# Sixteen ranks through four overlapped stages: VectorE's dependent steps in pieces of one link, attention scores over 32 rows, and a new order of the steps

## The reference

```python
x = x + jnp.tanh(g_xattn[0]) * _L0_xattn_ref(_layernorm(x, axis=-1), ctx_1024, mask_BxS2_bk0, ...)
x = x + jnp.tanh(g_ffn[0]) * _L0_ffn_ref(_layernorm(x, axis=-1), L0_ffn_w_gate, L0_ffn_w_up, L0_ffn_w_down)
x = x + jnp.tanh(g_xattn[1]) * _L1_xattn_ref(_layernorm(x, axis=-1), ctx_1024, ctx_1024, L1_xattn_Wq, ...)
x = x + jnp.tanh(g_ffn[1]) * _L1_ffn_ref(_layernorm(x, axis=-1), L1_ffn_Wr, L1_ffn_br, L1_ffn_W1, ...)
```

## Time and profile before

| | |
|---|---|
| median of 3 runs | 1644.17 us (1643.66 to 1647.43) |
| the profiled execution's own time | 1642.42 us |
| its span | 1640.8 us |
| TensorE, VectorE, ScalarE busy | 85%, 68%, 61% of the span |

### The profile page before, as it was taken

One profiled execution on the slowest core, in us unless ns is written; L12 is line 12 of the kernel. 1 busy time (PEld: TensorE's weight loads), 2 busy tenths in 40 slices (PEclk: granted clock), 3 DMA queues, 4 the chain that ended last, 5 costly groups with the idle time before them and its releaser, 6 DMA issues.

```text
span 1640.8 us, 35711 instructions
## 1 busy us (share of the span) xinstructions
PE 1400.4 (85%) x11645; PEld 1072.6 (65%) x11646; DVE 1117.3 (68%) x2887; ACT 993.4 (61%) x2861; POOL 413.3 (25%) x560
## 2 busy tenths in 40 slices
PE   2567789989999889989998671999999999999994
PEld 1445556665666566656664430888888888888883
DVE  7977779899988999899986534344444454444452
ACT  1244778888888888888876760444445444455542
POOL 0101011211122211212111112334433444344442
PEclk9587999999999999999999975999999999999997
DMA  6020132112320223203220005551231412322214
GB/s 192 13 87 30 62 103 103 45 61 104 103 92 21 95 104 103 72 33 104 94 94 8 8 14 179 177 162 32 33 112 30 114 32 35 108 35 32 35 31 123
DMA packets 63158, 123.58 MB, mean 75 GB/s; under 512 B 13955, under 2 KB 51967, under 8 KB 58879
## 3 DMA queue, kind: packets, MB, share of 16 engines
q1 hardware_dynamic: 45743, 102.75, 18.0%
q0 software_dynamic: 17312, 19.56, 7.2%
HBM read 78.64 MB, written 48.04 MB: 77 GB/s over the span
## 4 chain that ended last, share of the span: by engine, by line
PE 52%; DVE 32%; ACT 8%; issue 5%; DMA 2%; POOL 1%; SPq 0%; DVEq 0%; ACTq 0%; POOLq 0%
PE bank L1401 15%; PE bank L1403 14%; PE bank L1402 14%; DVE b_mn L1121 4%; ACT b_ex L746 3%; PE bank L1483 2%; PE bank L1495 2%; DVE wm L1238 1%; DVE f_hs L1182 1%; DVE split_room L1265 1%; DVE wm L1190 1%; PE bank L1719 1%; DVE x L1176 1%; DVE wm L1196 1%; DVE wm L1201 1%
## 5 line engine op out<-in xcount | busy, mean ns | idle before, releaser
L1401 PE MATMUL bank<-split_room,wm 128*128 128x256 f16 x1152 | 314.9, 273 | 8.2 <-issue 6.8
L1378 DVE SCALAR_TENSOR_TENSOR split_room<-bank,b12e,split_room 128x256 f32<-128x256 f32 x288 | 138.2, 484 | 265.6 <-ACT split_room L900 260.8
L1402 PE MATMUL bank<-split_room,wm 128*128 128x256 f16 x1152 | 314.8, 273 | 0.0
L1403 PE MATMUL bank<-split_room,wm 128*128 128x256 f16 x1152 | 314.7, 273 | 0.0
L900 ACT ACTIVATE split_room<-bank,b12e 128x256 f32<-128x256 f32 x288 | 134.2, 470 | 196.0 <-PE bank L1403 194.2
L746 ACT ACTIVATE b_ex<-bank,b_mn 128x120 f32<-128x120 f32 x512 | 177.0, 361 | 36.9 <-DVE b_mn L1121 28.0
L1403 PE MATMUL bank<-wm,split_room 128*128 128x256 f16 x576 | 157.0, 273 | 0.0
L1401 PE MATMUL bank<-wm,split_room 128*128 128x256 f16 x576 | 157.0, 273 | 0.0
L1402 PE MATMUL bank<-wm,split_room 128*128 128x256 f16 x576 | 157.0, 273 | 0.0
L692 POOL DMA_INDIRECT acc<-split_room,m_cur x72 | 116.1, 1612 | 133.0 <-ACT split_room L914 106.1
L1483 PE MATMUL bank<-b_k,b_q 128*128 128x480 f32 x256 | 131.8, 597 | 14.6 <-ACT b_q L834 14.6
(11 more groups left out here) (356 smaller groups left out, 3616.3 us busy)
## 6 DMA issues: line engine op xcount, KB each, us to landing
split_room<-in_L_ffn_W SPq DMA_DIRECT2D x48, 512.0 KB, 8.0
wsplit<-split_room SPq DMA_DIRECT2D x16, 1536.0 KB, 6.6
wm<-wsplit SPq DMA_DIRECT2D x16, 1536.0 KB, 8.5
acc<-x SPq DMA_DIRECT2D x17, 256.0 KB, 2.2
xin<-in_x SPq DMA_DIRECT2D x16, 256.0 KB
rows<-r_row SPq DMA_DIRECT2D x16, 256.0 KB, 3.7
ct<-in_ctx SPq DMA_DIRECT2D x16, 120.0 KB
cb<-in_ctx SPq DMA_DIRECT2D x16, 120.0 KB, 2.6
```

The source lines that it names most:

```text
L1378: dve.scalar_tensor_tensor(m_h[:, c % 3], bank[c % 4][:, TILE:2 * TILE], b12e[:, p, 1, c:c + 1], m_s[:, c % 2], ALU.add, ALU.mult).then_in ...
L1401: pe.matmul(o, lh, rh, start=start, stop=False)
L1402: pe.matmul(o, ll, rh, start=False, stop=False)
L1403: return pe.matmul(o, lh, rl, start=False, stop=stop)
```

## The change

**One link per step.** Chained steps are cut at each wait, and every piece is a step of its own that the tables can place: `variances` becomes `stats`, `moments` and `guard` (`B.ln`, `B.ln_1`, `B.ln_2`), the quantisation becomes `F.qa`, `F.qa_1`, `F.qa_2`, `F.qb`, `F.qc`, `F.qc_1`, `F.p`, `F.p_1`, the routing `R.logit` to `R.logit_5` and `R.rank_0` to `R.rank_5` (with `R.rank`, which only waits). The instructions and their waits stay as they are.

**Scores over 32 rows.** In B two rounds (of four heads each, in neighbouring groups of 32 rows of the array) are issued together, as four products of 32 rows and 240 columns that go to the two banks in turn. The channels of the heads are laid out in another order for this: `b_k` holds two copies of the keys in place of eight, `b_k_` writes it with two ScalarE instructions over 128 partitions instead of eight over 32, and the queries' and keys' weights and biases are permuted when they are split in the ramp (`prep_b`, `head_order`: 16 pieces of 64 elements per weight half and matrix in place of two of 512). The bias `bqk` comes with eight small transfers instead of one. Both banks must be free before a pair starts, and both minima wait for the pair's end.

**New tables.** All three tables are written anew for every engine.

```diff
-        b_k = sb("b_k", [P, NK, 2, QUAD, S])
+        b_k = sb("b_k", [P, NK, 2, S])
...
             "DVE": ...
-                "F.p/1 F.d1/2 A.p0/0 A.p1/0 B.rx1/3 F.t/1 W2/1 B.p7/3 B.ln/2 B.o1/3 A.ot/0 B.out/3 R.ln/3 F.gu0/1 A.out/0 "
+                "B.s4/2 F.ht1/1 B.s5/2 F.ln/0 A.s0/-1 F.ln_1/0 R.rank_2/3 F.ln_2/0 W0/0 B.s6/2 F.qa/0 B.rx0/2 F.qa_1/0 "
...
             def b_k_(b, p):
                 held(act, B.k_mm, b + 1)
-                for j in range(QUAD):
-                    h = slice(PITCH * j, PITCH * (j + 1))
-                    for a in range(2):
-                        last = act.activation(b_k[h, :, a, j], bank[2][h, 0:NK * S].rearrange("p (c s) -> p c s", c=NK), ACT.Copy, scale=C[h, C_M + a:C_M + a + 1])
+                for f in range(2):
+                    last = act.activation(b_k[:, :, f], bank[2][:, 0:NK * S].rearrange("p (c s) -> p c s", c=NK), ACT.Copy, scale=C[:, C_M + f:C_M + f + 1])
                 last.then_inc(B.k, 1)
...
                         w = (wq1, wk1, wv1, wo1)[n_ - 1]
-                        split(st1[:, n_ - 1], w[:, 0], w[:, 1])
+                        if n_ > 2:
+                            split(st1[:, n_ - 1], w[:, 0], w[:, 1])
+                            return
+                        for c in range(2):
+                            for a in range(2):
+                                for k in range(NK):
+                                    k_ = slice(k, k + 1)
+                                    split(head_order(st1[:, n_ - 1, k_], c, a, True)[:, 0],
+                                          head_order(w[:, 0, k_], c, a, False)[:, 0], head_order(w[:, 1, k_], c, a, False)[:, 0])
...
             def variances(G, ch, source):
-                def stage(b, p):
+                def stats(b, p):
                     ch.start(b)
                     dve.wait_ge(source.done, b + 1)
...
+                def moments(b, p):
+                    ch.go_on(b)
                     ch.hold()
...
+                def guard(b, p):
+                    ch.go_on(b)
                     ch.wait()
...
                 def minima(k):
                     def stage(b, p):
-                        dve.wait_ge(G.s_mm, b * n + k + 1)
+                        dve.wait_ge(G.s_mm, b * n + (k + 1 if G is A else k // 2 * 2 + 2))
...
+                def pair(b, k0):
+                    if k0 == 0:
+                        pe.wait_ge(B.q, b + 1)
+                        pe.wait_ge(B.k, b + 1)
+                    else:
+                        pe.wait_ge(B.exp, b * n + k0)
+                    for e in range(NK):
+                        for k in (k0, k0 + 1):
+                            t, r = k // per, k % per
+                            h = slice(PITCH * r, PITCH * (r + 1))
+                            last = pe.matmul(sbks[k % 2][:, e * 2 * S:(e + 1) * 2 * S], q[h, e, t * P:(t + 1) * P], kk[h, e], start=True, stop=True)
+                            if e == NK - 1:
+                                last.then_inc(B.s_mm, 1)
```

More of the change, by code:

```diff
@@ L369, in gated_stack @@
         FIRST = {
-            "SP": ("B.load@0 W@0 A.load@2 B.load@1 A.load@3 W@1 A.load@4 W@2 B.load@2 B.out@0 W@3 R.rank@0").split(),
-            "POOL": ("A.ln@0 A.ln@1 F.ln@0 A.ln@2 F.ln@1 B.ln@0 A.ln@3 F.ln@2 B.ln@1 R.ln@0 A.ln@4 R.scatter@0").split(),
[7 rows of a table removed]
-                "R.logit@0 A.t@4 B.s0@1 B.s1@1 F.a0@2 B.t0@1 B.s2@1 B.t1@1").split(),
[11 rows of a table removed]
-                "R.rank@0 A.rk@4 B.s3@1 F.q1c@2 F.p1@2 F.ht0@2 B.s4@1").split(),
[8 rows of a table removed]
-                "B.t0@1 B.s2@1 B.p0@1 R.rank@0 A.kv@4 B.t1@1 F.ht0@2 B.t2@1 B.s3@1 A.q0@4 A.q1@4 B.p1@1").split(),
+            "SP": ("W@0 A.load@2 B.load@0 B.load@1 A.load@3 W@1 W@2 A.load@4 W@3 B.load@2 B.out@0 B.load@3 R.rank@0").split(),
@@ L444, in gated_stack @@
+            "POOL": ("R.ln@13 R.scatter@13 B.ln@15 R.ln@14 R.scatter@14 R.ln@15 R.scatter@15").split(),
[6 rows of a table added]
+                "B.t6@15 B.t7@15 B.rx1@15 B.r7@15 B.o1@15 R.z@15 R.t@15 R.logit@15").split(),
[11 rows of a table added]
+                "R.rank_4@15 R.rank_5@15 R.rank@15").split(),
[6 rows of a table added]
+                "B.p4@15 B.t5@15 B.t6@15 B.p5@15 B.t7@15 B.p6@15 B.p7@15 B.out@15 R.t@15 R.logit@15 R.rank@15").split(),
         }
@@ L1122, in minima, with shares @@
                     return stage
-                def values(k):
+                def shares(k):
                     def stage(b, p):
@@ L1137, in rounds @@
                 if G is A:
-                    made.update({f"{G.name}.p{k}": values(k) for k in range(per - 1, n, per)})
+                    made.update({f"{G.name}.p{k}": shares(k) for k in range(per - 1, n, per)})
+                    made.update({f"{G.name}.p{k}_1": values(k) for k in range(per - 1, n, per)})
                 return made
@@ new lines, in f_scale, with stage, f_inverse @@
+            def f_scale(n):
+                v, m, sc = F_PARTS[n]
+                def stage(b, p):
+                    cf.go_on(b)
+                    cf.wait()
+                    cf.link(dve.tensor_scalar(sc[:, 0], sc[:, 2], SIXTH, 1e-12, ALU.mult, ALU.max))
+                return stage
+            def f_inverse(n):
+                v, m, sc = F_PARTS[n]
+                def stage(b, p):
+                    cf.go_on(b)
+                    cf.wait()
+                    dve.reciprocal(sc[:, 1], sc[:, 0]).then_inc(F.v, 1)
+                return stage
@@ L1228, in f_q, with f_unscale, stage @@
+            def f_unscale(n):
+                v, m, sc = F_PARTS[n]
+                def stage(b, p):
+                    cf.go_on(b)
+                    cf.wait()
+                    dve.tensor_tensor(blocks(v), blocks(v), over(sc[:, 0], BLK), ALU.mult).then_inc(F.hq, 1)
                 return stage
```

221 lines of the change are left out of this document (137 added, 84 removed), and 127 rows, old and new, of tables (FIRST, LAST, ORDER).

## The result

The changed kernel takes 1674.85 us (median of 4 runs, 1670.34 to 1679.93) against 1644.01 us before: a ratio of 1.0184, with an interval of 1.0151 to 1.0216. It became slower, by 1.5 to 2.2%; 1575 us were forecast, and the range ended at 1603. The profiled execution has a span of 1673.7 us. The first rows are from its page: TensorE's clock in 40 slices, and the engines' shares of the chain that ended last.

What follows compares the result with a forecast made beforehand. VectorE was taken as the bound of the repeated part. Repetitions 39.5, ramp 11, drain 13 and changeover 6 us sum to 69.5 off the 1640.8 us span: 1571.3, plus 3.4 for the median, 1575 us; range 1555 to 1603.

Steps and rivals of the forecast that it cites:

- The links: Repeated part: an instruction waiting for its VectorE forerunner costs 0.12 us more; 24 such waits removed, 3.2 us per repetition.
- 49.9 - 3.2: VectorE's work and links per repetition, 49.9 us, less 2.9 for 24 links and 0.3 for four holding the sequencer.
- What is late next: Walk through one new repetition with old durations: waits of 1.7 and 0.3 us, repetition 48.7 us, eleven save 39.5.
- The wait for `f_z`: VectorE's `F.qa` waits for ScalarE's `f_z` behind three GpSimd operations: 1.7 us per repetition, between 0.8 and 2.5.
- The scores: B's score products overlap in row groups: 3.2 us less per repetition, 0.8 back; TensorE from 47.9 to 45.5 us.
- Rival 2: B's scores: row groups don't run side by side; repetition about 49.8 us, kernel 1592 us, chance 0.14.
- ScalarE's 2.4 us: Saved by two `b_k_` instructions for eight; hidden in the repeated part, worth about 1 us at the last rank.
- Ramp and drain: Ramp -11 us, between +5 and -22; drain -13 us, between -5 and -20.
- rival 3: Ramp: the weight pieces eat what the new order gains; 1586 us, chance 0.13.
- Half of it overlaps with the transposes: Drain: score pairs save 1.5 us for each of 8, 12 at most; half overlaps, so 6 us.
- The changeover: Before the experts: last split weights written some 6 us sooner, shrinking two waits; -6 us, between 0 and -10.
- (4): Slower: score pairs take the banks, their 2 us turns stand open on VectorE; up to 1663 us, chance 0.04.

Runs made afterwards that it cites:

- the wide form: Changed kernel with the scatter moved one repetition on and seven useless products per repetition, but scores over 128 rows (480 columns, masked keys): 1706.36 us.

## Why the prediction was wrong

**The links: the mechanism right, the exact hit in part luck.** Work and links are 46.8 us in the changed kernel and 46.4 to 46.6 in its variants, 46.7 were forecast, and putting 17 links back costs 2.1. But both numbers of 49.9 - 3.2 were too high. The 2.4 us of waits left out two rows of the view of the earlier trace rows:

```profile
DVE b_o L1152 <- ACT b_o L779: 0.3, 1, 0.3
DVE r_pair L1318 <- DVE r_w L1314: 0.2, 1, 0.2
```

Over the eleven repetitions before, VectorE waits 31.3 us, 2.85 each, so that its work and links were 49.4 us. The change saved 49.4 - 46.8 = 2.6 us, 0.11 for each of 24 links; the 0.3 us for four that "also hold the sequencer" had no row, and no run shows them. The Trainium skill (VectorE: DVE Perf Modes, Rules for kernel authors) advises to minimise operations and not semaphores; here a pair of neighbours that wait for each other costs 0.12 us, and where VectorE is the bound it counts.

**What is late next: the step that failed.** I forecast 1.7 + 0.3 = 2.0 us of waits per repetition from a walk with the old durations, and they were 7.4: eleven times 5.4 is 60 of the 102 us between the span forecast (1571.3 us) and measured (1673.7). Two things were missing in the walk. First, it took a signal to arrive when the work ends. Beside the scatter TensorE's signals come up to 2.7 us late (2.2 us of VectorE's 7.4 at `a_zt`), and the new table has the scatter beside `A.ot`, for which ScalarE, VectorE and TensorE wait in turn. The old trace has what looks like the same sign (507.19 above), but there the scatter cost at most 0.9 us. Second, it took TensorE's clock as given. That TensorE falls to 45.5 us, under VectorE's 48.7, was meant as harmless; the late signal and the shorter work left TensorE waits of 2.0 and 1.2 us, and the clock fell behind both. With the scatter moved and the waits filled, a repetition takes 49.1 us: the 48.7 that I had forecast, with 2.75 us of waits in place of 2.0. The wait for `f_z` that I had at 1.7 us is 0.9; GpSimd's three operations ahead of it take 2.0 us in place of 2.9 (515.83 to 517.86 us), as forecast, but in that repetition 0.6 us of the time are spent one step earlier, at a minimum that waits for TensorE (517.51 us).

The split of the 5.0 us between 54.2 and 49.1: moving the scatter gives 3.1 (of which part is the clock's first fall), the products that hold the clock another 1.9. Alone, the clock's part is 2.8 us (the run with 14 products).

**The scores: the overlap right, `b_k_` wrong.** A pair takes 1.01 us; I had 0.8 + 0.2 (that the 0.2 are changes of the row count no run shows). Rival 2 falls: its sign, pairs of 1.6 us, did not come. The runs with 480 columns over 128 rows are not rival 2 itself, since they also bring back the eight instructions of `b_k_`. They cost 6.2 us per repetition where rival 2 had 1.1, and ScalarE's 2.4 us, which I had costed at nothing, lie on the way to `b_q`, to the first pair and to `a_zt`.

**Ramp and drain: both wrong, one hidden by the other.** `A.out` is a poor mark, since the new table moves it against B. Here is `B.out` of ranks 1 and 12, before and after, on VectorE:

```profile
269.53 0.69 DVE L1176 TENSOR_TENSOR x<-x,bank 128x512 f32<-128x512 f32 x1 [0.77 <-PE bank L1403]
```

```profile
844.67 0.69 DVE L1176 TENSOR_TENSOR x<-x,bank 128x512 f32<-128x512 f32 x1 [0.77 <-PE bank L1403]
```

```profile
270.51 0.69 DVE L1244 TENSOR_TENSOR x<-x,bank 128x512 f32<-128x512 f32 x1 [0.69 <-PE bank L1533]
```

```profile
866.64 0.69 DVE L1244 TENSOR_TENSOR x<-x,bank 128x512 f32<-128x512 f32 x1 [0.89 <-PE bank L1533]
```

Cut there, the ramp is 1.0 us longer (rival 3, the ramp gives nothing, was true), the eleven repetitions 21.0 and the drain 9.6 us longer, and from the last routing step on it is 1.4 us: together the 32.9 us by which the span grew. Against the forecast (11, 39.5, 13 and 6 us less) they miss by 12, 60, 23 and 7 us, the 102 us in all.

Of the drain's 9.6 us, 2.8 lie between `B.out` of ranks 14 and 15 (45.8 against 43.0 us), and the products without a use, which raise the clock there from 0.57 to 1.00, give them back. In that run the three distances between rank 15's four pairs save 3.6 us in all, and round 7's minimum loses them again. The other 6.8 us lie between `B.out` of ranks 12 and 14 (104.2 against 97.4 us). There the kernels with five products and with those of the drain too take 102.5 and 103.1 us, so that more products give nothing back; what costs these 5 to 7 us stays open. "Half of it overlaps with the transposes" had no row behind it.

**The changeover: wrong.** The write was issued 5.9 us sooner against the last routing step, as forecast (2.2 us ahead of its start in place of 3.7 behind it). What failed is that its landing would come sooner too: issued 1.7 us behind the first expert's load, it took 19.4 us, where it had taken 12.0 when it was issued 7.5 us behind. GpSimd waits for it (`W.out`) as VectorE does, and reads its list of tokens at 1046.76 us, 18.0 us behind the start of the last routing step in place of 16.7. The gain of 6 us was a loss of 1.

**The rivals.** (4), slower, named the banks, and the turns of the pairs were not it: VectorE waits 11.6 / 11 = 1.1 us per repetition for scores, against 0.9 before. It had the right sign by another mechanism. The sum of chances on "faster", 0.94, left no room for a cause outside the walk, though two engines within 3 us of the bound give such causes their weight.

## What to carry on

A walk through a new order with old durations finds the work and the dependences, in this case to 0.6 us per repetition; it doesn't find what a step does to its neighbours in time. Before trusting it, list in the old trace every wait whose releaser had ended well before ("remote", or a named releaser as at 507.19), see what ran beside it, and follow where the new order puts that. And give the engine that is relieved something to do, or price its clock: here a kernel with 1.5 us of useless products per repetition is faster than one without.

## What the runs showed of the hardware

- While GpSimd issues the four indirect transfers of a scatter (5.0 us), TensorE's signals to ScalarE and VectorE arrive up to 2.7 us late, though its work goes on and it takes VectorE's signals in time (`F.gu0` starts at 528.01, 0.06 us behind the subtraction it needs). In two kernels the late step starts 0.9 and 0.3 us behind the end of the last transfer's issue (530.80 behind 529.92, 542.70 behind 542.38). The delay moves with the scatter, and is not seen at `A.ot` when two of the four transfers are left out. Why it is so stays open.
- TensorE's granted clock fell to 1.2 GHz behind stretches in which it waited 2.0 us once, or 1.2 us in two pieces, with transposes between them and products of 8 columns ahead; with products of 128 columns in the waits it stayed at 2.4 GHz for 540 us. In the wide form, where TensorE waits 2.9 us for `b_q`, it fell once per repetition in spite of the same products. The Trainium skill (TensorE: Matmul & The Clock Gate, HAM oscillation) tells of the same for waits between groups of products. How many falls come differs between executions: 7, 5 and 1 in the eleven repetitions of three kernels that have the same tables there.
- Products over 32 rows in different row groups overlap: 1.01 us for two times 480 columns of f32, 1.62 for the two over 128 rows, and 0.81 would be half.
